# Feed-forward of a 256-token chunk between the attention steps, and query-key products on four column quarters

## The reference, cut to what matters

```python
x = layernorm(x + attention(x))
h = gelu(ternary_linear(x, w_up))       # 128 -> 512, input divided by its rms
x = layernorm(x + ternary_linear(h, w_down))  # 512 -> 128, h divided by its rms
```

## Time and profile before

| | |
|---|---|
| median of three runs | 281.09 us |
| the profiled execution | 283.06 us, its span 280.6 us, mean granted clock 0.947 |
| busy: PE, DVE, ACT, POOL | 239.9, 179.2, 149.7, 92.3 us |
| scores of step 0 begin | 25.76 us |
| PE ends the last step's `c_part` | 203.6 us |
| last result written by DVE / end of the span | 274.5 / 280.6 us |

### The profile page before, as it was taken

How to read it: one execution, slowest core, us unless ns; L and a number is a source line. 1 busy time by engine, 2 the same in 40 slices (tenths; PEclk the granted TensorE clock), 3 DMA queues, 4 the chain that set the end, 5 groups by cost and what they waited for, 6 DMA issues and landing times. The chain is left out here.

```text
span 280.6 us, 6720 instructions
## 1 busy us (share of the span) xinstructions
PE 239.9 (85%) x2722; PEld 213.2 (76%) x2722; DVE 179.2 (64%) x409; ACT 149.7 (53%) x292; POOL 92.3 (33%) x137
## 2 busy tenths in 40 slices
PE   1899949999999999999999999999987769659430
PEld 1898839989998999899989998998877647537310
DVE  0364764877765776577657765778775566984731
ACT  1374335676565656565656565546351587596400
POOL 8023211242242241242144125125113275654420
PEclk9999977999999999999999999999997998997875
DMA  7742740001001002002002001000000000001011
GB/s 231 207 115 69 218 107 0 2 16 44 2 20 40 0 2 57 6 0 60 2 0 58 4 2 39 21 2 0 2 2 0 0 1 2 27 12 36 1 39 37
DMA packets 16370, 10.43 MB, mean 37 GB/s; under 512 B 1812, under 2 KB 15700, under 8 KB 16212
## 3 DMA queue, kind: packets, MB, share of 16 engines
q1 hardware_dynamic: 15760, 8.96, 11.0%
q10 hardware_dynamic: 580, 1.05, 1.2%
HBM read 7.86 MB, written 2.10 MB: 35 GB/s over the span
## 5 line engine op out<-in xcount | busy, mean ns | idle before, releaser
L419 POOL TENSOR_TENSOR E<-E,rc 128x400 f32<-128x400 f32 x32 | 27.5, 859 | 125.8 <-DVE rc L746 125.8
L716 DVE TENSOR_TENSOR CTl<-bank,CTh 128x512 fp32r<-128x512 f32 x64 | 41.1, 684 | 29.8 <-ACT CTh L481 29.8
L481 ACT ACTIVATE Yb<-bank 128x512 f32<-128x512 f32 x64 | 37.8, 591 | 33.2 <-PE bank L876 32.7
L481 ACT ACTIVATE CTh<-bank 128x512 fp32r<-128x512 f32 x64 | 34.7, 595 | 22.5 <-PE bank L989 22.5
L874 PE MATMUL bank<-xTh,Gh 128*128 128x256 f32 x128 | 39.3, 307 | 0.4 <-DVE Gl L664 0.4
L874 PE MATMUL bank<-CTh,Mh 128*128 128x256 f32 x128 | 37.1, 290 | 2.1 <-DVE CTl L716 2.1
L1025 PEld LDWEIGHTS bank<-xT,Yb 128*64 128x64 f32 x1024 | 33.2, 140 | 5.8 <-issue 5.2
L1025 PE MATMUL bank<-xT,Yb 128*64 128x50 f32 x1024 | 37.3, 227 | 0.4 <-DVEq L725 0.4
L875 PE MATMUL bank<-CTl,Mh 128*128 128x256 f32 x128 | 36.5, 285 | 0.0
L876 PE MATMUL bank<-CTh,Ml 128*128 128x256 f32 x128 | 36.4, 284 | 0.0
L875 PE MATMUL bank<-xTl,Gh 128*128 128x256 f32 x128 | 36.3, 284 | 0.0
(11 more groups left out here) (129 smaller groups left out, 448.8 us busy)
## 6 DMA issues: line engine op xcount, KB each, us to landing
raw<-in_L_attn_x SPq DMA_DIRECT2D x36, 64.0 KB
w_sb<-in_L_attn_w_qkv ACTq DMA_DIRECT2D x2, 512.0 KB, 5.8
pt_rows<-PT SPq DMA_DIRECT2D x1, 1024.0 KB, 5.5
R<-pt_rows SPq DMA_DIRECT2D x1, 1024.0 KB, 5.5
out<-outS SPq DMA_DIRECT2D x4, 192.0 KB
raw<-in_L_attn_x SPq DMA_DIRECT2D x12, 56.0 KB
xq<-in_L_attn_x SPq DMA_DIRECT2D x2, 256.0 KB, 5.7
w_sb<-in_L_attn_w_qkv SPq DMA_DIRECT2D x1, 512.0 KB, 6.6
```

The costliest lines, as they stand in the source:

```text
L419: nc.gpsimd.tensor_tensor(e, e, rc[j % 2][:, :].unsqueeze(2).broadcast_to([P, TILES, WIN]), ALU.mult).then_inc(s_norm, 1)
L481: copy = lambda o, i, **k: nc.scalar.activation(o, i, ACT.Copy, **k)
L716: v.tensor_tensor(ct_view(CTl[par], sc, bk), c_view(bk), ct_view(f32(CTh[par][:, :, :]), sc, bk), ALU.subtract).then_inc(s_CTl, 1)
```

## The change

One loop over 32 steps `s` replaces `I` and `j`. From step 10 on, each group of four steps (`n, k = ffn(s)`, k = 0 to 3) carries the feed-forward of chunk `n` (256 tokens) piece by piece on all engines; chunks 5 (its rest), 6 and 7 follow after step 31. Features stay on partitions in the hidden layer: `wuT` is stationary, gelu writes [features, tokens] and is not transposed; high parts are made on DVE, low parts and squares on POOL, and the sums of squares over features come from matmuls with a column of ones. Input is normalised ahead of the up product (`x1n`), so gelu has no scale. All feed-forward products of a chunk use one PSUM bank (F_BANK, bank 1) in turn, so the scores have one bank (bank 0), and AT has one buffer. Query-key products are made in four quarters of 32 stationary columns. ACT adds the bias while it copies the O bank. `xq` is loaded again per chunk (`xr`), results are stored per chunk from `y2`. The fills of the first steps are ordered anew.

```diff
-        IN_STEP = [[("a", 0, 6, "D"), ("v0", 0, 7, "D")],
-                   [("bos", 0, 6, "D"), ("x", 2, 5, "AD"), ("x", 3, 7, "AD")],
-                   [], [], [], []]
-        IN_STEP[T_STEP] += [("t", 0, 4, "A"), ("t", 1, 6, "D")]
+        IN_STEP = [[("a", 0, 1, "D"), ("v0", 0, 7, "D")],
+                   [("x", 2, 1, "AD"), ("bos", 0, 7, "D")],
+                   [("t", 0, 1, "A"), ("t", 1, 7, "D")],
+                   [("m", 0, 7, "AD"), ("m", 1, 1, "AD")],
+                   [("m", 2, 7, "AD"), ("m", 3, 1, "AD")],
+                   [("x", 3, 1, "AD")]]
...
+            def scores(s):
+                need(pe, s_sub, s)
...
+                    for lo in range(0, P, 32):
+                        mm(bank[S_BANK][lo:lo + 32, WIN * tile:WIN * tile + WIN], Yb[s // 4 % 2][:, ytile, lo:lo + 32], keys,
+                           start=(tile == 0), stop=False, skip_group_check=True)
...
+            def attn_back(n):
+                pe.wait_ge(f_stage, n + 1)
+                if n < 6:
+                    need(pe, f_y2, CT * n)
...
+            def up(n, t):
+                pe.wait_ge(f_xTl, n + 1)
+                need(pe, f_gelu, 2 * n + (t if n < 5 else 0))
...
+            def down(n):
+                if n < 5:
+                    pe.wait_ge(f_gelu, 2 * n + 2)
+                for k in range(FT):
+                    pe.wait_ge(f_gl, 2 * n + k // 2 + 1)
...
+            def down_back(n):
+                pe.wait_ge(f_dS, n + 1)
+                pe.wait_ge(f_sum, 2 * n + 2)
...
+                        for lo in range(0, P, 32):
+                            ins = mm(dn_bank(n)[lo:lo + 32, CHUNK + i:CHUNK + i + 1],
+                                     gT[n == 6][:, 2 * t, P * i + lo:P * i + lo + 32], ones[:, 0:1],
+                                     start=(t == 0), stop=(t == 1), skip_group_check=True)
```

More of the change, by code:

```diff
@@ new lines, in next_window @@
+            def next_window(c):
+                sp.wait_ge(s_xwl, c)
+                window(*divmod(c, 2))
+            residual_rows(0)
+            for c in range(1, CHUNKS):
+                next_window(c)
+                if c >= 5:
+                    store(c - 5)
+                if c >= 3:
+                    residual_rows(c - 2)
+            store(CHUNKS - 5)
+            residual_rows(CHUNKS - 2)
+            store(CHUNKS - 4)
+            residual_rows(CHUNKS - 1)
+            for n in range(CHUNKS - 3, CHUNKS):
+                store(n)
@@ new lines, in _ @@
+            dve.wait_ge(s_eps, 1)
+            for s in range(STEPS):
+                n, k = ffn(s)
+                if k == 1 and n > 0:
+                    result(n - 1)
+                if k == 2:
+                    x1_lo(n)
+                if k == 3:
+                    hidden_high(n, 0)
+                if s == LAG + 1:
+                    dve.wait_ge(s_pt, 16)
+                if s > LAG:
+                    ct_lo(s - LAG - 1)
+                if s >= LAG:
+                    at_lo(s - LAG)
+                if k == 0 and n > 0:
+                    hidden_sum(n - 1)
+                if k == 1:
+                    up_input(n)
+                if k == 3:
+                    hidden_high(n, 1)
+                shift(s)
+                if k == 0 and n > 0:
+                    second(n - 1)
+                total(s)
+                if s < len(IN_STEP):
+                    fills(IN_STEP[s])
+                if s == 0:
+                    ternary()
+                if k == 0:
+                    residual(n)
+                if k == 1:
+                    layernorm(n)
@@ new lines, in _ @@
+            x1_lo(5)
+            ct_lo(29)
+            at_lo(30)
+            residual(6)
+            hidden_high(5, 0)
+            hidden_high(5, 1)
+            up_input(6)
+            ct_lo(30)
+            at_lo(31)
+            x1_lo(6)
+            layernorm(6)
+            ct_lo(31)
+            hidden_sum(5)
+            second(5)
+            hidden_high(6, 0)
+            hidden_high(6, 1)
+            result(5)
+            hidden_sum(6)
+            second(6)
+            residual(7)
@@ L868, in _ @@
+            up_input(7)
+            x1_lo(7)
+            layernorm(7)
+            result(6)
+            hidden_high(7, 0)
+            hidden_low(7, 0)
+            hidden_high(7, 1)
+            hidden_low(7, 1)
+            hidden_sum(7)
+            second(7)
+            result(7)
         @block.tensor
@@ new lines, in _ @@
+            transposes(30)
+            pe.wait_ge(s_Ye, 64)
+            up(5, 0)
+            up(5, 1)
+            pe.wait_ge(s_sub, STEPS)
+            attn_back(6)
+            c_part(30)
+            transposes(31)
+            x1_T(6)
+            c_part(31)
+            down(5)
+            up(6, 0)
+            up(6, 1)
+            o_part(7, 0)
+            o_part(7, 1)
+            down_back(5)
+            o_part(7, 2)
+            down(6)
+            o_part(7, 3)
+            down_back(6)
@@ L1151 @@
+            pe.wait_ge(s_ATl, STEPS)
+            attn_back(7)
+            x1_T(7)
+            up(7, 0)
+            up(7, 1)
+            down(7)
+            down_back(7)
 _INS = ["L0_attn_x", "L0_attn_w_qkv", "L0_attn_w_out", "L0_attn_b_out", "L0_attn_w_th", "L0_ffn_w_up", "L0_ffn_w_down"]
```

978 lines of the change are left out of this document (442 added, 536 removed).

## The result

The changed kernel takes 297.86 us (median of 4 runs, 297.8 to 299.46) against 280.57 for the kernel before: ratio 1.063, 95% interval 1.058 to 1.068. It is 17 us slower; the forecast was 285, 4 slower. The profiled execution took 297.8, its span is 295.7.

A forecast was written before the change was run, and what follows sets the result against it. PE was taken to bound attention steps at 5.60 us, a chain through all engines the filled ones. Start 81.8, filled steps 146.3 and tail 56.4 make 284.5; with 2.4 outside, less 2.0 to the median, 285; range 266 to 300.

The forecast's parts named there:

- The ring: Chain of waits through ACT, DVE, POOL and PE in four filled steps: 27.4 us a chunk against PE's 24.4.
- Rival A: Steps 10 to 31: PE keeps the pace, the ring is slack; 24.4 us per four steps, time 269; chance 0.28.
- signs of being wrong: Prediction wrong if steps from 10 hold 6.1 us, the score block grows, or the tail stays above 62.
- the tail: From PE's end of step 31 to the span's end: 56.4 us against 77.0, -20.6; bounds 52 and 60.
- the quarters: Score block of each step in four column quarters: 0.80 us instead of 1.08, -0.28 a step.
- rival B: Score blocks: each quarter instruction as dear as now, +1.28 us a step against the forecast; time 307 to 322; chance 0.12.
- the table changes: ACT alternates exponential and gelu in filled steps: two table loads a chunk at 1.28 us each.
- rival C: Table change in mid-stream costs up to its own length again, 2.6 us a chunk in the ring: 299; chance 0.07.
- rival D: Half clock in steps 2 and 3 goes and the tail is 3 us shorter: 279; chance 0.07.
- PE's own work: PE in four filled steps: 21.3 us with quarters, 24.4 with the feed-forward's matmuls, transposes and small sums.
- the filled steps: Steps 10 to 31: 24.8 us first chunk, 82.2 next three, 26.2 fifth, 13.1 last two steps; 146.3 in all.
- steps 0 to 9: Earlier fills -2.0 us, quarters -2.2, later x block on DVE +1.0; step 10 begins at 81.8, bounds 78 and 93.

The follow-up runs named there:

- Experiment 2: Changed kernel with scores again as 32 matmuls of 64 columns instead of 64 of 32: 299.36 us, ratio 1.073.
- experiments 3 and 4: Changed kernel, 3 with a plain copy for the gelu (no table loads): 293.36 us; 4 with POOL's squares cut to two columns: 285.73 us.
- experiment 1: Kernel before with only its scores changed, to 64 matmuls of 32 columns: 271.74 us, ratio 0.974.
- experiment 9: Changed kernel with POOL taking the second low part ahead of the squares in step k3: 298.74 us, ratio 1.070.
- experiment 10: Changed kernel with POOL's squares(5,0) in the tail waiting until DVE has done x1n of chunk 6: 295.87 us, ratio 1.061.
- experiment 8: Changed kernel with 292 idle matmuls ahead of PE's waits in the tail, to hold the granted clock: 295.76 us, ratio 1.059.
- experiment 7: Changed kernel with squares at two columns, relu for gelu and layernorm (L796) at two columns: 284.54 us, ratio 1.017.

## Why the prediction was right and wrong

**Right: what sets a filled step.** The ring was put at 27.4 a chunk; it measured 28.07, 27.93 and 27.93. Experiment 2 shows that PE does not set it, experiments 3 and 4 that pieces the prediction put on the ring are on it. PE's waits came where they were named, but smaller: x1n 0.2 to 0.4 and x1Tl 0.5 a chunk, where above 0.5 was named as the sign, and the low part 0.9. Rival A (PE keeps pace) is refuted. Of the signs of being wrong one came true: the tail stayed above 62, at 62.7.

**Right: the quarters.** 0.85 a block, 0.23 saved, 0.28 forecast; rival B is refuted, and experiment 1 shows that what the edit is worth alone, 7.2 us, is mostly lost behind the ring.

**Right: the table changes** cost their 1.28 and no more, against rival C. The drain of the Trainium skill (ScalarE: Activation LUTs, "What ACT_TABLE_LOAD costs") is not in the trace: the gelu starts 0.01 to 0.02 us behind the load in mid-stream too, and the load as closely behind the Y copy. The half clock in steps 2 and 3 (32.4 to 39.3) stayed, so rival D did not come about either.

**Off in size: PE's own work.** Four steps with quarters 21.3, measured 21.4; but the feed-forward adds 4.2 to them (25.6 busy), not 3.1. It was not the bound, so it cost little by itself, but it left only 2.3 us to gain by mending the ring.

**Wrong: the filled steps, +6.2.** First chunk 26.2 for 24.8, three chunks 83.9 for 82.2, fifth 29.4 for 26.2, last two steps 13.0 for 13.1. The step that failed is the durations taken for two pieces of DVE's work: the second `hidden_high` at 0.42 and `layernorm` at 0.6. Where they run beside POOL they measured 0.92 and 1.10, each chunk again: L807 is held by the squares, L796 by the multiplication. That is 1.0 a chunk, of which links priced too high made up half. That these holds set the chunk's length is read from the timeline, where L807, the maximum, the subtraction and the exponential follow one another within 0.04; no run took them away alone (experiment 9 did for L807, and POOL's own queue took its place). Of the fifth chunk's 3.2 some 2.0 are the half clock (216.8 to 223.6), as step 29 of experiment 2 shows, 8.98 for 11.00 with the same wait of PE for the second low part, 2.3 us. The sum had no half clock there, and the wait only at the rate of the covered chunks (measured 0.9). What set the clock off stays open, since that run waited as long. Both only moved time between the stretches: the tail's chain began no later for them (experiment 9).

**Wrong in size: steps 0 to 9, +1.4.** No run was made for this. From the mask product of step 3 to that of step 7 it took 22.4 us against 20.8 before, where the sum had one read of an x block, +1.0, less the quarters' 1.1; which part of the new order of fills makes up the difference stays open.

**Wrong: the tail, +6.3.** By the prediction's landmarks from PE's end of step 31: root of chunk 6 at 8.4 (8.5 forecast); `up_input(6)` done at 13.3 instead of 9.7 (8.5 and its own 1.2), of which 3.5 is DVE held by POOL (experiment 10 took 2.5 of it away); `down_back(5)` starts at 23.6 instead of 17.4, so +2.7 more: `c_part(31)` took 1.65, and `down(5)` and `up(6)` 3.6 at half clock, where the sum had them covered. From there on the forecast intervals hold within 0.7: last result at 57.1 for 50.2. The steps that failed here are DVE's durations and "PE at the lower clock adds little, it is seldom last": experiment 8 puts the clock's share at 1.3 or more, and the rest of the 2.7 is read from the timeline.

**The missing rule.** The prediction allowed "POOL slowed beside DVE" as a bound and never the reverse: DVE held by POOL. The Trainium skill (SBUF — State Buffer, "Who interferes with whom") says that the two engines share a pair of ports as an exclusive lock, taken by a DVE copy, cast or `tensor_scalar` in a two-port mode, or by a DVE instruction with two SBUF inputs against one of GpSimd that reads SBUF, and that whoever starts second blocks until the first is through. The traces agree: in the tail seven of DVE's instructions, of 1 to 128 columns, end 0.02 to 0.08 us behind one of POOL's, the casts of 512 columns in mid-stream 0.29 behind (158.28 + 0.92 against 157.87 + 1.04), while those that read PSUM (L739 681 ns, L744 681) and the sums (L759 570) measure the same beside POOL and alone. One case is milder than the rule: beside POOL's power functions of 2 or 4 columns, 0.7 to 1.0 us long, L847 and L783 keep 0.34 and 0.22.

Almost all SBUF-to-SBUF work of DVE in the kernel before runs alone or beside such small power functions, so the rows taken gave its price alone. But its trace has one case that I passed over: of the two `tensor_scalar` of 512 columns at L706 one took 0.89 beside POOL's multiplication, the other 0.47 without. DVE's timeline there, then POOL's:

```profile
30.59 0.89 DVE L706 TENSOR_SCALAR tern<-w_ff,tsum 128x512 f32<-128x512 f32 x1
```

```profile
30.34 0.86 POOL L419 TENSOR_TENSOR E<-E,rc 128x400 f32<-128x400 f32 x1 [1.44 <-DVE rc L746]
```

## What to carry to other kernels

Work moved to an idle engine is not free when its instructions hold up those of the engine on the chain: list, for each new wide instruction on POOL, which SBUF-to-SBUF instructions of DVE run at that time, and price those at what is left of POOL's, however small they are. The same goes for a test that cuts such an instruction down: look in its trace whether it became shorter. When steps are filled until a second chain is as long as the bound, stop counting idle shares and sum the chain; here the filled steps paid 34 us for a tail shortened by 14. An edit that shortens the bound engine (the quarters) should be timed alone, since it may be worth more without its companion. And count a tail from an event on its own chain: counted from PE's last mask product, experiment 10 showed half of what its wait had brought.

## What the runs showed of the hardware

- Matmuls of 32 stationary columns on four column quarters start 13 ns apart on average (0.85 us for 64: three starts 5 to 8 ns apart, the next group 24 to 28 ns later); of 64 columns on two halves 34 ns (1.08 for 32). The least spacing of 25 ns in the Trainium skill (TensorE: Matmul & The Clock Gate, "Wait — 56ns, not 53.3ns?") does not hold across column quarters.
- DVE's two one-column instructions took 2.21 us beside POOL and 0.34 alone. Of `tensor_scalar` beside POOL's multiplication, 128 columns took 0.89 and 2 columns 0.90 (L796, changed kernel and experiment 7).
- The granted clock fell to half in mid-stream in one profiled execution of experiment 9 (138.9 to 142.3), after PE had waited 1.3 for the squares; it waited as long in the other chunks at the full clock, so what set it off stays open. In the changed kernel it fell at 216.8, after a wait of 2.3 us in step 29; in experiment 2 the same wait was followed by the full clock.
